# Seven instead of six superblocks of layer one from dense products

## The reference

```python
h = jnp.maximum(_layernorm(x, axis=-1), 0.0)
h = h @ lin_w.T + lin_b
for i in range(3):
    m = h @ weight[i]
    agg = jax.ops.segment_sum(m[src], dst, num_segments=n_nodes)
    h = gru_cell(agg, h, w_ih, w_hh, b_ih, b_hh)
return x + h
```

## Time and profile before

| what | value |
|---|---|
| median of 3 runs | 4353.29 us (4349.5 to 4356.58) |
| the profiled execution | 4358.24 us, of which its span is 4356.8 |
| TensorE busy | 3251.4 us (75%) |
| GpSimd busy | 3195.4 us (73%) |
| VectorE busy | 2734.1 us (63%) |
| ScalarE busy | 2594.7 us (60%) |
| main memory traffic | 1039.46 MB, 239 GB/s |
| L547, gathers on GpSimd | 3168, 992 ns each |
| L839, dense products | 7448, 1645.0 us busy |
| L821, counting products | 5376, 720.8 us busy |

### The profile page before, as it was taken

How to read it: one execution, slowest core, us unless ns; L and a number is a source line. 1 busy time by engine, 2 the same in 40 slices (tenths; PEclk the granted TensorE clock), 3 DMA queues, 4 the chain that set the end, 5 groups by cost and what they waited for, 6 DMA issues and landing times.

```text
span 4356.8 us, 76088 instructions
## 1 busy us (share of the span) xinstructions
PE 3251.4 (75%) x24940; PEld 2780.4 (64%) x24941; DVE 2734.1 (63%) x7740; ACT 2594.7 (60%) x3881; POOL 3195.4 (73%) x3230
## 2 busy tenths in 40 slices
PE   6277777777777678776888788888768787877775
PEld 4155555555555567675777777777767777776774
DVE  7455555565656566665666666666656666666664
ACT  5155655565656566665666666666655665665662
POOL 4777777777777777745777777777667777777776
PEclk8588888888988788888988889998888888998887
DMA  8388888888888987777777777777967777777774
GB/s 269 108 232 225 231 230 230 225 232 228 233 227 232 281 269 252 257 239 229 248 257 250 258 242 264 251 258 247 295 210 237 252 240 250 240 252 238 253 237 133
DMA packets 782766, 1039.46 MB, mean 239 GB/s; under 512 B 91560, under 2 KB 656936, under 8 KB 782376
## 3 DMA queue, kind: packets, MB, share of 16 engines
q1 hardware_dynamic: 515064, 645.79, 45.2%
q0 software_dynamic: 152064, 311.63, 25.2%
q10 hardware_dynamic: 115248, 77.10, 5.6%
HBM read 783.68 MB, written 250.48 MB: 237 GB/s over the span
## 4 chain that ended last, share of the span: by engine, by line
POOL 72%; issue 22%; PE 3%; DMA 1%; DVE 1%; ACT 0%; DVEq 0%; POOLq 0%; ACTq 0%; SPq 0%
POOL ring_region L547 72%; PE psum L839 1%; DMA ring_region<-messages,edge_src 1%; PE psum L737 0%; PE psum L730 0%; PE psum L747 0%; DVE aggT L942 0%; PE psum L794 0%; POOL ring_region L530 0%; DMA messages_region<-in_x 0%; ACT wide_counts L664 0%; DMA messages<-pieces_out 0%; POOL ring_region L528 0%; DVE bn L923 0%; ACT aggT L587 0%
## 5 line engine op out<-in xcount | busy, mean ns | idle before, releaser
L547 POOL DMA_INDIRECT ring_region<-messages,edge_src x3168 | 3141.3, 992 | 1069.8 <-issue 964.7
L664 ACT CAST wide_counts<-messages_region 128x864 fp32r<-128x864 f16 (+1 forms) x1596 | 1540.9, 1031 | 401.4 <-PE psum L839 380.6
L839 PE MATMUL psum<-wide_counts,message_halves 128*128 128x432 f32 x7448 | 1645.0, 380 | 0.0
L839 PEld LDWEIGHTS psum<-wide_counts,message_halves 128*128 128x128 f32 x7448 | 1475.6, 200 | 85.2
L806 PE MATMUL psum<-onehot,ring_region 128*128 128x36 bf16 x9504 | 318.3, 184 | 908.5 <-DMA ring_region<-messages,edge_src 900.9
L806 PEld LDWEIGHTS psum<-onehot,ring_region 128*128 128x128 bf16 x9504 | 286.0, 100 | 1006.7 <-issue 997.7
L687 ACT CAST messages_region<-psum 128x504 f16<-128x504 f32 x1344 | 685.3, 609 | 210.1 <-PE psum L821 184.3
L1255 DVE TENSOR_TENSOR message_halves<-messages_region,message_halves 128x256 fp32r<-128x256 f32 (+1 forms) x1596 | 751.9, 471 | 55.0
L821 PE MATMUL psum<-messages_region 128*128 128x238 bf16 (+2 forms) x5376 | 720.8, 291 | 63.6 <-ACT messages_region L687 45.6
L1253 DVE CAST message_halves<-messages_region 128x256 fp32r<-128x256 f32 (+1 forms) x1596 | 615.2, 385 | 157.0 <-PE psum L839 155.6
L821 PEld LDWEIGHTS psum<-messages_region 128*128 128x128 bf16 x5376 | 517.7, 108 | 249.2 <-issue 57.7
(11 more groups left out here) (103 smaller groups left out, 1671.4 us busy)
## 6 DMA issues: line engine op xcount, KB each, us to landing
messages_region<-counts SPq DMA_DIRECT2D x532, 768.0 KB
counts<-messages_region SPq DMA_DIRECT2D x1344, 128.0 KB
ring_region<-messages,edge_src POOLq DMA_INDIRECT x3168
messages<-pieces_out ACTq DMA_DIRECT2D x98, 192.0 KB
messages_region<-plain SPq DMA_DIRECT2D x21, 896.0 KB, 10.1
temps<-states ACTq DMA_DIRECT2D x98, 128.0 KB
states<-temps ACTq DMA_DIRECT2D x98, 128.0 KB
plain<-temps ACTq DMA_DIRECT2D x98, 128.0 KB
```

What stands on the lines that cost most here:

```text
L547: nc.gpsimd.indirect_dma_start(out=rows[:, n % RING, h * QC + c, :], out_offset=None, in_=messages[layer], in_offset=bass.IndirectOffsetOn ...
L664: nc.scalar.copy(wide_counts[:, v % UBUF, :, cols], stage[v % ABUF][:, :, cols]).then_inc(s_wide, 1)
L839: mm = nc.tensor.matmul(psum[:, 6 + kg % 2, 0:DQ * W], halves[:, v % UBUF, b % HB, half * P:(half + 1) * P], wide_counts[:, v % UBUF, :, c ...
```

## The change

One constant is changed. `FIRST_DENSE` is the share of layer one's superblocks that is taken in dense form: `KD` goes from 6 to 7, `KG` from 10 to 9, `TURN` from 130 to 117. All that is counted stays; its 1344 rounds are shared out over the steps up to the new `TURN`. The steps of layer one go from 172 to 166. Nothing else in the code is changed.

```diff
-FIRST_DENSE = 3 / 8
+FIRST_DENSE = 7 / 16
```

## The result

| | before | after |
|---|---|---|
| median | 4351.40 us (4348.26 to 4356.58, 4 runs) | 4290.47 us (4278.01 to 4296.40, 4 runs) |
| profiled execution | 4358.24 us | 4278.01 us |
| ratio | | 0.9852, interval 0.9834 to 0.9869 |

What follows compares the result with a forecast made beforehand. GpSimd's string of gathers was taken as the bound. Thirteen steps fewer (130.3 us) less seven dense ones more (72.4 us) gain 58 us: 4353.3 - 58 = 4295 us, range 4284 to 4319.

Steps and rivals of the forecast that it cites:

- The bound: Whole kernel: GpSimd's string of 3168 gathers sets the time, 72% of the chain; GpSimd never waits for TensorE.
- The seven dense steps: Layer one gains seven steps with dense products, at 10.34 us each: 72.4 us more.
- The thirteen removed steps: Layer one loses 13 steps that gather and count, each worth 10.02 us: 130.3 us less.
- hold-ups: Counting steps of layer one: 44 us of gather time above 10.02 us a step belongs to counting and stays whole.
- Counting at no cost: Layer one: 1344 rounds in 109 steps instead of 122, 12.3 a step for 11.0, add nothing to the path.
- The cover: Counting steps: TensorE's wait for gathered rows hides the denser counting, 1.5 us a step left, near 163 us in all.
- DMA: Counting steps: packets take 991 of 1137 us, a share of 87% instead of 82%, without slowing the gathers.
- The rival with a ceiling at 0.82: Counting steps: DMA share can't pass 82%, so 1208 us for 109 steps, +15 us, 4368 us in all; chance 0.05.
- The queues and the first dense tile: Layer one: denser stores on SP, loads still behind them, first dense tile still seven steps after TURN; no new wait.
- The end of layer one: Gap of 75 us between layer one's last gather and layer two: no change, some 5 us either way by luck.
- Counting step of 10.40 to 10.45 us: Sign in layer one that the forecast is right; 10.38 us or less would speak for the average price.
- the average price: Rival: hold-ups go with the steps, so each removed counting step is worth 10.38 us; gain 62.5 us, 4291 us; chance 0.22.

Runs made afterwards that it cites:

- the second trace: The changed kernel measured and traced again, unchanged, on a usual chip: 4289.63 us against 4352.79 for the kernel before, ratio 0.9855.
- the packed kernel: Kernel before with BUILD_SPARE 15 instead of 2: counting packed into steps 6 to 114, no steps cut; 4351.23 us against 4352.79, ratio 0.9998.
- the first trace: The profiled execution of the changed kernel in the result table: 4278.01 us, the fastest of its four runs.
- eight: FIRST_DENSE 8/16 instead of the changed kernel's 7/16, 96 counting steps; on a usual chip 4245.87 us, ratio 0.9763 to the kernel before.
- nine: FIRST_DENSE 9/16 instead of the changed kernel's 7/16, 83 counting steps; on a usual chip 4192.41 us, ratio 0.9640 to the kernel before.
- ten: FIRST_DENSE 10/16 instead of the changed kernel's 7/16, 70 counting steps; 4251.95 us against 4360.87 for the kernel before, ratio 0.9753.
- seven: The changed kernel itself, FIRST_DENSE 7/16 where the kernel before has 3/8: 4290.47 us against 4351.40, ratio 0.9852.

## Why the prediction was right, step by step

- **The bound.** Right on the chip of the result: no wait of GpSimd for TensorE, chain unchanged. Not a property of the kernel, though: on one of the chips used the same program is held up at TensorE's sums, at 13.9 us a counting step.
- **The seven dense steps**, 72.4 us: measured 72 (434 to 507 us), and the same price of 10.34 us a step; the second trace had 10.37.
- **The thirteen removed steps**, 130.3 us: the packing alone shows 10.03 us a step without counting, which is the term itself (10.02). The stretch gave more in the first trace, 141 us, and 136 in the second. The difference is in the hold-ups. I took them as 44 us and as staying whole; counted over 10.02 us a step they were 33 and 38 us in the two traces of the change and 38 in the packed kernel. Before's 44 us held three gathers of 3.09 us, 6.4 us over the usual 0.945, which the change doesn't show. The gathers of the counting steps, first before and then after, ns shortest, median and longest:

```profile
L547 POOL DMA_INDIRECT ring_region<-messages,edge_src x976: 942/947/3094, 189.0 to 1453.9; - x196
```

```profile
L547 POOL DMA_INDIRECT ring_region<-messages,edge_src x872: 942/946/1427, 189.1 to 1313.0; - x175
```

  Without these few the hold-ups did stay whole. Here they are for each trace of a usual chip with all counting in it, as the time by which gathers of 1 to 2 us exceed 0.945 us:

| kernel | counting steps | hold-ups, us |
|---|---|---|
| before | 122 | 37.8 |
| change, two traces | 109 | 33.0, 38.6 |
| packed | 109 | 38.1 |
| eight | 96 | 33.7 |
| nine | 83 | 38.1 |
| ten | 70 | 37.0 |

  Shared out per step, 70 steps would have had 22 us of them. So the mechanism was right. The size was some 6 us too large, because I read three rare gathers as a part of what stays; whether they appear is chance. 58 forecast, 61 measured, and 63 the second time.
- **Counting at no cost.** Right, and shown by the packed kernel (ratio 0.9998). The cover was mis-sized: TensorE's wait for rows was to fall to 163 us and fell to 196.5, as TensorE needed 869 us of busy time and not the 911 or so that I carried over from before. Of these 42 us, 24 are the counting products (713 us before, 689 after), shorter at the higher granted clock. Most of the rest, 17 us, is in the products of tiles, of which the shorter stretch has 26 for 29; I hadn't taken those three off.
- **DMA.** 0.87 forecast, 0.88 and 0.87 measured. The rival with a ceiling at 0.82 is out: nine reaches 0.97. At that share its first sign does show: ScalarE waits 90.4 us for stores there, 16.5 before.
- **The queues and the first dense tile** cost nothing to be seen. The end of layer one took 73 and 76 us for 75.
- **Counting step of 10.40 to 10.45 us**: missed, it was 10.32 and 10.37. By the sign that I had set, this would have spoken for the average price; the packed kernel shows that it doesn't. A sign that lies inside the scatter of two executions decides nothing.
- **The range**, 4284 to 4319, held the median; three of its four runs lie in it.

## What to carry to other kernels

A step that is pulled by one engine is worth what that engine needs for it undisturbed; what neighbours add stays as long as the neighbours' work does. Measure that by moving the neighbours' work away and leaving the steps, which costs one constant. Cover should be looked for until it ends: here two more superblocks of the same change still paid, 44 and 53 us, and the third gave about as much back. Where two engines are tied by a ring, the ring is cover as well, but only for a stretch that ends before it is full. And a gain that rests on one engine's slack should be timed on more than one chip.

## What the runs showed of the hardware that I had not expected

One chip runs the same program 20% slower (5203 against 4351 us), though the gathers' records (987 ns in the mean of the counting steps, 993 before), ScalarE's copies (583 ns, 609) and VectorE's L1217 (646 ns, 655) are as short as on the usual one. What waits for TensorE's products starts late: the copies by 0.72 us after the modelled end in the median (0.09 in the kernel before on the usual chip), and a tenth of them by over 4.3 us. The lengths of TensorE's records show little of it (315 ns a counting product in the mean, 292 before); the start of what waits for them does. The cause isn't known.

TensorE's products of the same counting work became shorter as the rest was packed more tightly, 292 to 273 ns in the mean, while its granted clock went from 0.86 to 0.97. Busy time carried over from a stretch with a lower granted clock came out too high for seven, 911 us for 869. Nine's counting still took 11.1 us a step, as forecast, as waits took the place of busy time.

A few gathers took 3.09 us instead of 0.945, three in the counting steps before and five in those of eight, none in those of seven, nine and ten. The traces show no cause.
